# Second layer's head: moments, cleared buffers and first weight loads made in the stage in front, lone rows taken second

## What is computed

```python
x = x + L1(_gn(x), weight_real, weight_imag)

def _gn(v, G=32, eps=1e-5):                 # v seen as (B, H, W, C): C is the last axis, 128 wide
    g = v.reshape(B_, H_, W_, G, C_ // G)   # 32 groups of 4 columns
    m = jnp.mean(g, axis=(1, 2, 4), keepdims=True)
    s = jnp.var(g, axis=(1, 2, 4), keepdims=True)
    return ((g - m) / jnp.sqrt(s + eps)).reshape(v.shape)

def L1(x, wr, wi):
    weight = complex(wr, wi)                # (32 in, 32 out, 128, 65)
    x_ft = symmetric_padding(rfftshift(rfft2(x)))
    out_ft = einsum('bixy,ioxy->boxy', x_ft, symmetric_padding(weight))
    return irfft2(irfftshift(out_ft))
```

## Time and profile before

| what | value |
|---|---|
| device time, median of 3 runs | 1035.99 us (1034.77 to 1037.75) |
| device time of the profiled execution | 1040.15 us |
| its span in the profile | 1038.4 us |
| PE, DVE, ACT, POOL busy | 793.5, 677.6, 405.6, 319.4 us |
| stage 7 | 564.6 to 664.0 us |
| stage 8, head | 664.0 to 681.5 us |
| stage 8, loop | 681.5 to 957.6 us |
| stage 8, tail | 957.6 to 1038.4 us |
| mean granted clock of PE | 0.912 |

### The profile page before, as it was taken

The page is one execution under the profiler, slowest core; times in us unless marked ns, Lnnn a source line. Parts: engine busy times, 40 slices in busy tenths (PEclk is TensorE's granted clock), DMA queues, the critical chain, the costliest instruction groups (busy, mean ns, idle before and its releaser), DMA issues. The chain is left out here.

```text
span 1038.4 us, 37308 instructions
## 1 busy us (share of the span) xinstructions
PE 793.5 (76%) x16319; PEld 588.8 (57%) x16319; DVE 677.6 (65%) x1446; ACT 405.6 (39%) x919; POOL 319.4 (31%) x201
## 2 busy tenths in 40 slices
PE   0399496989999837999914999468777777776897
PEld 0366242222222217888703999457777777776786
DVE  4898499788888793566658999745555555552122
ACT  0199352222222263556533566333333333331121
POOL 0022375789999701111100000322222232210000
PEclk9999697999999978999956999888989899898899
DMA  9566643665556230554131676589999999998677
GB/s 366 110 188 174 139 90 108 242 219 170 196 161 194 86 79 22 167 125 117 39 75 40 167 200 176 117 180 252 287 283 289 283 283 281 286 283 175 197 235 218
DMA packets 284674, 189.45 MB, mean 182 GB/s; under 512 B 29397, under 2 KB 275894, under 8 KB 283382
## 3 DMA queue, kind: packets, MB, share of 16 engines
q1 hardware_dynamic: 207411, 139.95, 50.0%
q10 hardware_dynamic: 75138, 44.14, 16.9%
q0 software_dynamic: 2048, 4.36, 2.0%
HBM read 154.50 MB, written 33.07 MB: 181 GB/s over the span
## 5 line engine op out<-in xcount | busy, mean ns | idle before, releaser
L2101 PE MATMUL po<-pa,room 128*32 128x16 f32 x8320 | 146.6, 219 | 69.3 <-DMA room<-_L_conv_weight_imag_dram 44.7
L2101 PEld LDWEIGHTS po<-pa,room 128*32 128x32 f32 x8320 | 144.3, 162 | 76.9 <-issue 65.5
L1051 POOL TENSOR_TENSOR q<-lead 128x1536 f32<-128x1536 f32 (+1 forms) x49 | 163.5, 3364 | 19.7 <-PE acc L1088 17.0
L1134 DVE TENSOR_TENSOR q<-pw,lead 128x1536 f32<-128x1536 f32 (+1 forms) x84 | 139.0, 1703 | 15.8 <-PE acc L1088 13.9
L2054 POOL COPY cols<-y 128x512 f32<-128x512 f32 x32 | 36.8, 1149 | 326.3 <-PE px L2088 184.8
L1088 PE MATMUL acc<-q,pt 128*32 128x384 f32 (+1 forms) x1080 | 102.9, 493 | 12.2 <-DVE q L1134 12.2
L2242 DVE TENSOR_TENSOR osl<-po,neg 128x128 f32<-128x128 f32 x64 | 18.4, 288 | 132.9 <-ACT neg L2175 132.9
L2175 ACT ACTIVATE neg<-po 128x272 f32<-128x272 f32 x32 | 12.7, 398 | 180.5 <-issue 167.2
L2088 PE MATMUL px<-wbat,cols 128*32 128x130 f32 x2176 | 75.9, 291 | 3.7 <-DVE wbat L2213 3.0
L1088 PEld LDWEIGHTS acc<-q,pt 128*32 128x32 f32 x1080 | 27.9, 110 | 84.3 <-issue 54.8
L1446 PE MATMUL pz<-eh,ts 128*33 128x128 f32 x1024 | 66.3, 285 | 6.1 <-DMA ph<-const_ph_dram 3.8
(11 more groups left out here) (353 smaller groups left out, 1547.5 us busy)
## 6 DMA issues: line engine op xcount, KB each, us to landing
room<-_L_conv_weight_real_dram ACTq DMA_DIRECT2D x32, 520.0 KB, 8.6
room<-_L_conv_weight_imag_dram ACTq DMA_DIRECT2D x32, 520.0 KB, 11.3
room<-_L_conv_weight_real_dram SPq DMA_DIRECT2D x32, 520.0 KB, 6.4
room<-_L_conv_weight_imag_dram SPq DMA_DIRECT2D x32, 520.0 KB, 9.8
lead<-xns SPq DMA_DIRECT2D x64, 192.0 KB, 3.0
lead<-wv SPq DMA_DIRECT2D x16, 576.0 KB, 5.8
yall<-in_x_dram SPq DMA_DIRECT2D x4, 2048.0 KB, 14.6
xd<-in_x_dram SPq DMA_DIRECT2D x16, 512.0 KB, 4.1
```

Of the source, the lines that this page charges most:

```text
L1051: nc.gpsimd.tensor_tensor(q2[:, t % 2, :, :, 0:m], bc(weights(blk, n), 2, NB), spectra(blk), ALU.mult).then_inc(s_qp, 1)
L1134: V.tensor_tensor(q1[:, t % 2, :, :, 0:m], bc(pw[t % 4][:, 0:3 * m].rearrange("p (r m) -> p r m", r=3), 2, NB), spectra(blk), ALU.mult).th ...
L2101: e = nc.tensor.matmul(po[u][32 * g:32 * g + 32, 512 * q + 16 * m:512 * q + 16 * m + 16], wsl[u][:, :, q * KWF + KWF - 1 - kw], xsl[u][:, ...
```

## The change

Six edits, all in stages 7 and 8.

1. **Moments.** ACT's two sums of squares of a group now cover other elements: one the two columns 0 and 64 (16 elements a lane), one the rest (1008 elements a lane, scaled by the root of 2). Their accumulators then need only be added. At the end of stage 7 DVE makes both moments with two reductions; the ten steps of stage 8 are gone, and the factor 1/32 is in the constant `gmean`.
2. **Cleared buffers.** POOL clears `xsl` in stage 7, after the last `s_q7`.
3. **Matrices.** SP loads `gmean` and `wide` at the start of stage 7, ahead of that stage's own loads.
4. **First loads.** SP issues three of the eight first weight loads in stage 7, after the last read of `tt`; the other five follow at the start of stage 8, three on SP and two on ACT.
5. **First columns.** ACT instead of POOL copies the columns of the first chunk, one half on each side of its square root, and then issues its two loads; POOL copies those of the second chunk after `s_b0`.
6. **Order.** The chunk with the lone rows is taken second instead of last (`TURN8`).

```diff
+TURN8 = (0, NCHK - 1) + tuple(range(1, NCHK - 1))
...
-    c["gmean"] = (n[:, None] // 4 == n[None, :] // 4) / 4.0
+    c["gmean"] = (n[:, None] // 4 == n[None, :] // 4) / (4.0 * NT)
...
+        def load_weights(eng, p, c_, parts=(0, 1)):
+            u, k = c_ % 2, TURN8[c_]
+            if p == 1:
+                row0, step = HH // 2 - SL * (k + 1), 1
+            elif k < NCHK - 1:
+                row0, step = HH // 2 + 1 + SL * k, 1
+            else:
+                row0, step = HH // 2, HH // 2 - 1
...
             def _(sp):
+                for t, n in ((gmean, "gmean"), (wide, "wide")):
+                    sp.dma_start(t[:, :], c[n]).then_inc(s_ld, 16)
                 each_batch(body)
+                sp.wait_ge(s_ts, NGRP)
+                load_weights(sp, 0, 0)
+                load_weights(sp, 1, 0, (0,))
+
+            @block.gpsimd
+            def _(pool):
+                pool.wait_ge(s_q7, NGRP)
+                for v in range(2):
+                    nc.gpsimd.memset(xsl[v], 0.0).then_inc(s_zero, 1)
...
-                    act.activation(sq7[:, 0], y1[:, bass.ds(g * GI, GI), 0:64], ACT.Square, accum_out=en8[:, 0, bass.ds(g, 1)])
-                    act.activation(sq7[:, 1, :, 0:63], y1[:, bass.ds(g * GI, GI), 66:129], ACT.Square, accum_out=en8[:, 1, bass.ds(g, 1)]).then_inc(s_sq7, 1)
+                    act.activation(sq7[:, :, 126:128], y1[:, bass.ds(g * GI, GI), 0:65:64], ACT.Square, accum_out=en8[:, g, 0:1])
+                    act.activation(sq7[:, :, 0:126].rearrange("w i (s k) -> w i s k", s=2), y1p[:, g * GI:g * GI + GI, :, 1:64], ACT.Square, scale=ROOT2,
+                                   accum_out=en8[:, g, 1:2]).then_inc(s_sq7, 1)
...
+                dve.wait_ge(s_e1, NGRP)
+                V.reduce_sum(mo[:, 0, :], y1[:, :, 0].rearrange("w (b i) -> w b i", b=NB), axis=AX.X)
+                dve.wait_ge(s_sq7, NGRP)
+                V.reduce_sum(mo[:, 1, :], en8[:, :, :].rearrange("w (b q) s -> w b (q s)", b=NB), axis=AX.X).then_inc(s_mo8, 1)
...
             def _(sp):
-                for t, n in ((gmean, "gmean"), (wide, "wide")):
-                    sp.dma_start(t[:, :], c[n]).then_inc(s_ld, 16)
...
-                for c_ in range(NCHK):
+                load_weights(sp, 1, 0, (1,))
+                load_weights(sp, 0, 1)
+                for c_ in range(2, NCHK):
                     wait(sp, s_ms, c_ - 1)
                     load_weights(sp, 0, c_)
...
             def _(pool):
+                for c_ in range(1, NCHK + 2):
                     wait(pool, s_sp, c_ - 1)
                     if c_ < NCHK:
-                        near = y1v[:, SL * c_ + 1:SL * c_ + 3]
-                        if c_ == NCHK - 1:
+                        if c_ == 1:
                             pool.wait_ge(s_b0, 1)
...
             def _(act):
-                load_weights(act, 1, 0)
+                near, far = columns(0)
+                act.activation(cols[:, 0, 0:2], far, ACT.Copy)
+                root.serve(act, nc.scalar, gs[:, 2, :])
+                act.activation(cols[:, 0, 2:4], near, ACT.Copy).then_inc(s_col0, 1)
                 load_weights(act, 1, 1)
-                root.serve(act, nc.scalar, gs[:, 2, :])
                 act.wait_ge(s_zero, 2)
...
             def _(dve):
-                ch.link(V.reduce_sum(mo[:, 0, :], y1[:, :, 0].rearrange("w (b i) -> w b i", b=NB), axis=AX.X))
-
-                ch.link(V.tensor_tensor(sq[:, :, :], y1[:, :, 0:65:64], y1[:, :, 0:65:64], ALU.mult))
-                ch.link(V.reduce_sum(en2[:, :, :], sq[:, :, :].rearrange("w (b i) k -> w b k i", b=NB), axis=AX.X))
...
-                V.tensor_scalar(mo[:, :, :], mo[:, :, :], 1.0 / NT, None, ALU.mult).then_inc(s_mo8, 1)
...
-                    last = c_ == NCHK - 1
+                    last = TURN8[c_] == NCHK - 1
```

More of the change, by code:

```diff
@@ L1976, in build, with columns @@
             block = p8.enter_context(nc.Block())
+            y1v = y1[:, :, :].rearrange("w i (s k) -> w k s i", s=2)
+            def columns(c_):
+                k = TURN8[c_]
+                near = y1v[:, SL * k + 1:SL * k + 3]
+                return near, near if k < NCHK - 1 else y1v[:, 0:64:63]
             xob = xo.rearrange("(b o) h w -> h b o w", b=NB)
             yb = yall[:, :, :].rearrange("h (b o) w -> h b o w", b=NB)
[L1980 to L1996, removed]
             @block.sync
             def _(sp):
-                for t, n in ((gmean, "gmean"), (wide, "wide")):
-                    sp.dma_start(t[:, :], c[n]).then_inc(s_ld, 16)
                 def store_pairs(c_):
-                    u = c_ % 2
+                    u, k = c_ % 2, TURN8[c_]
                     sp.wait_ge(s_oc, c_ + 3)
@@ L2043, in _ @@
             def _(pool):
-                y1v = y1[:, :, :].rearrange("w i (s k) -> w k s i", s=2)
-                def columns(c_):
-                    u = c_ % 2
+                for c_ in range(1, NCHK + 2):
                     wait(pool, s_sp, c_ - 1)
                     if c_ < NCHK:
-                        near = y1v[:, SL * c_ + 1:SL * c_ + 3]
-                        if c_ == NCHK - 1:
+                        if c_ == 1:
                             pool.wait_ge(s_b0, 1)
-                        nc.gpsimd.tensor_copy(cols[:, u, 0:2], near if c_ < NCHK - 1 else y1v[:, 0:64:63])
-                        nc.gpsimd.tensor_copy(cols[:, u, 2:4], near).then_inc(s_col, 1)
-                    else:
-                        nc.gpsimd.memset(cols[:, u, 0, 0, 0:1], 0.0).then_inc(s_col, 1)
-                columns(0)
-                columns(1)
-                for v in range(2):
-                    pool.wait_ge(s_col, 2)
-                    wait(pool, s_zero, v)
-                    nc.gpsimd.memset(xsl[v], 0.0).then_inc(s_zero, 1)
-                pool.wait_ge(s_zero, 2)
-                for c_ in range(NCHK):
-                    columns(c_ + 2)
+                        near, far = columns(c_)
+                        nc.gpsimd.tensor_copy(cols[:, c_ % 2, 0:2], far)
+                        nc.gpsimd.tensor_copy(cols[:, c_ % 2, 2:4], near).then_inc(s_col, 1)
+                    else:
+                        nc.gpsimd.memset(cols[:, c_ % 2, 0, 0, 0:1], 0.0).then_inc(s_col, 1)
             @block.tensor
@@ L2074, in _, with spectrum @@
                 pe.wait_ge(s_wb, 1)
-                def spectrum(c_, u):
-                    pe.wait_ge(s_col, c_ + 1)
+                def spectrum(c_, u, first=False):
+                    if first:
+                        pe.wait_ge(s_col0, 1)
+                    else:
+                        pe.wait_ge(s_col, c_)
                     for q in range(SL):
@@ L2103, in mix @@
                     e.then_inc(s_ms, 1)
-                spectrum(0, 0)
+                spectrum(0, 0, True)
                 spectrum(1, 1)
```

53 lines of the change are left out of this document (27 added, 26 removed).

## The result

The changed kernel takes 1031.12 us against 1039.45 us of the kernel before (medians of 10 runs each, taken in turn on the same chip; 1025.9 to 1034.5 and 1034.8 to 1041.5). The ratio is 0.992 with a 95% interval of 0.9901 to 0.9939: 8.3 us less, between 6.3 and 10.3. A second session gave 0.9941 (0.9919 to 0.9963), 6.1 us less. Forecast were 9.2 us less. The 1035.99 of the first three runs was low for the kernel before, so the forecast time, 1026.8, lies 4.3 under the measured one although the difference of the first session fits.

The account below looks back on a forecast made before the run. The prediction took a chain of waits as the bound: the loop's DMA time is fixed, its start hangs on PE's first mix. 7.0 us at the head plus 2.2 at the end, 9.2, takes 1035.99 to 1026.8; range 1022.2 to 1032.2.

Parts of the forecast that it names:

- Stage 7's end: End of stage 7: new squares +0.05 us and DVE's sum +0.21, so stage 8 starts 0.26 later.
- the row of the scaling: Profile row of DVE's scaling held up by POOL's memset; applied to stage 7's last add, it means 1.8 us later.
- The three early loads: Weight loads moved into stage 7's idle DMA stretch: 5.3 us at 295 GB/s, worth nothing themselves but cover for the rest.
- The head: Start of stage 8 up to mix(0): 6.56 us from the group sum plus 0.45 from silent POOL, 7.0 earlier.
- The rival in which the clock stays up: Head of stage 8: PE's clock does not fall, mix(0) comes 1.8 us earlier, total 1025.0; chance 0.07.
- the wait for `s_b0`: POOL's new wait before copying chunk 1's columns: ready about 670.3, 0.9 us before spectrum(1) can start, so no delay.
- The first pass of the loop: From mix(0) on: everything that follows comes earlier by as much as mix(0) does, 7.0 us.
- an "issue" hole over 2 us in mix(0): Listed sign that the forecast is wrong: PE standing still in mix(0) over 2 us for reasons the profile calls issue.
- PE stalls longer in the first pass: Rival: code-fetch holes around mix(0) grow by 2.6 and 1.8 us, gain only 4.8, total 1031.2; chance 0.13.
- The loop's end: Last weight wait before mix(31): shorter by 1.5 to 4 us with the lone rows second, taken as 2.2.
- The shortening below an ordinary wait: Loop's end: last loads have the DMA engines to themselves, so the wait may come at most 2.2 us below ordinary.
- The change of pace: Rival: loop steps slow from 8.45 us, at 8.77 no gain is left, priced at 1045.2 total; chance 0.08.

Follow-up runs that it names:

- e8: Kernel before with only the moments changed and the two small matrices loaded in stage 7; ratio to the kernel before 0.9973.
- e1: Changed kernel with the order undone, so the chunk with the lone rows is last again; ratio to the kernel before 0.9957.
- e7: Changed kernel with the weight loads of chunks 1 and 2 cut to a thin strip, leaving DMA nearly idle; one run, read-back at 287.70 us.
- the repeat: Changed kernel measured again unaltered, in a second session; ratio to the kernel before 0.9941, read-back at 294.20 us.
- e2: Changed kernel with the moments undone (old squares, ten DVE steps in stage 8), POOL still silent there; ratio to the kernel before 0.9927.
- e5: Changed kernel with only POOL's two memsets put back at the start of stage 8; ratio to the kernel before 0.9933.
- e4: Changed kernel with six of the eight first weight loads in stage 7 instead of three; ratio to the kernel before 0.9944.
- e9: e8 with one line moved: ACT answers the root before its two loads of chunk 1; ratio to the kernel before 0.9958.
- e6: Changed kernel with five of the eight first weight loads in stage 7 instead of three; ratio to the kernel before 0.9932.
- e3: Changed kernel with the three early loads put back into stage 8, all on SP's queue; ratio to the kernel before 1.0047.

## Why the prediction was right, and where it was not

**Stage 7's end: right in sum.** Forecast was +0.26 for the start of stage 8, with the group sum at once behind it. The stage started 0.07 later and the group sum 0.2 after that, so that it gained 6.57 where 6.56 was forecast: two misses of 0.2 that cancel. The memsets cost DVE's add nothing, as forecast for its operand in PSUM; by the row of the scaling it would have been 1.8. This agrees with the Trainium skill, "SBUF — State Buffer", section "Who interferes with whom", by which such a DVE instruction does not collide with a GpSimd instruction that only writes SBUF. ACT's copies of the columns took 1.16 each, not 0.60; the forecast took the time of a read of adjacent values. They stayed covered. The three early loads took about 10 us (645.7 to 656) where 5.3 was forecast, since one queue alone reached about 180 GB/s and not 295; the idle stretch was long enough for that too.

**The head: right in size, with two terms that were luckier than argued.** 7.22 against 7.0 at the start of mix(0); the 0.2 is the group sum at the higher clock, which the forecast did not have. The rival in which the clock stays up did not come. But the forecast said nothing of ACT's queue, which e8 shows to be the first thing that a quick head runs into; the change takes it out by its edit 5, which I had costed at nothing. And it had costed the wait for `s_b0` by what it delays (right, it delays nothing) and not by what it keeps away from DVE (1.1, e1).

**The first pass of the loop: the step that failed.** The sum took the 7.0 at mix(0)'s start over to its end. It is 4.64 there and 5.0 behind mix(1), and the forecast's own sign of being wrong, an "issue" hole over 2 us in mix(0), came with 3.10. The rival "PE stalls longer in the first pass" had the mechanism at twice the size (4.4 more; measured 1.06 and 3.10 instead of 1.87, 2.3 more), with a chance of 0.13. That was too low: rows of before showed a short hole with idle and a long one with busy DMA engines, and the forecast itself kept them busy to 676 or later, over the middle of mix(0). The forecast did not have the second part of the loss, the lower clock behind the longer stall. The page of the Trainium skill that has code streaming ahead of use and mostly hidden ("Runtime: NRT & Kernel Launch", section "Instruction fetch mechanics") is not borne out in this first pass: even with idle DMA engines PE stands still four times for 0.9 to 1.7 us (e7).

**The loop's end: right side, too small.** 2.2 forecast, 2.8 by all kernels together and 3.6 in the pair compared; the difference of the two waits (1.8) is what the last wait gave (1.7). The shortening below an ordinary wait, which the forecast allowed for by the bytes, did not come in that wait (11.2, an ordinary one); the other 1.0 lies one step earlier and was not forecast.

**The loop itself: right.** From mix(1)'s end on, the gain is kept. The change of pace did not come: from the loads of chunk 3 to those of chunk 30 a step takes 8.41 before and 8.40 after.

**The sum.** 7.0 + 2.2 = 9.2 was forecast; 5.0 + 3.6 = 8.6 is what the profile shows up to the read-back, 8.1 in the repeat, and 8.3 and 6.1 the time of whole runs. So the sum is near because one term was 2 us too large and the other 0.6 too small (1.4 in the pair compared): that is luck. One slip stands in the chances: of the 0.08 for another pace half was put past the point of no gain, but 0.06 was then counted as slower. Left open: whether the tail is 1 us longer with the lone rows second. It takes 76.9 to 82.4 us there (80.2 on the mean of eight) and 78.3 to 79.7 (79.0 on the mean of four) in the others.

## What to carry to other kernels

When a chain of small steps on the way to a DMA-bound loop is cut short, ask what the next engine in line will be doing at the new time: here ACT was issuing loads into a full queue, PE then waited for the loads, and then, by the reading above, for its own code, and each had been hidden by the slow chain. The moments were worth 1.9 on the kernel before (e8) and 2.3 or less on the changed one (e2), the clears 0.5 or less (e5); the whole head brought 5. The early loads were not measured by themselves. And a wait of one engine can be worth its while for what it keeps that engine from doing beside another.

## What the runs showed of the hardware

- Each of PE's stalls in the first pass that was looked at ends 2.2 to 2.9 us after one packet of 0.02 MB on an instruction queue is moved (before, after, e2, e4, e9); with idle DMA engines it is 2.2 to 2.4 (e7). With idle DMA engines such a stall is 0.9 to 1.7 us in this loop's first pass (e7); with weights in flight up to 4.7 (e2).
- Behind a stall of 3.10 us PE's granted clock was 0.57 (after); behind one of 1.87 it stayed at 1.00 (before).
- A DVE step of 0.16 us on few values, with two operands in SBUF or as a scaling, waits for the end of a POOL copy (up to 1.05 us, e1 and e8); beside a memset the scaling waits (0.67, e5) and the step with two SBUF operands doesn't (0.16, e5). For two SBUF inputs the Trainium skill says the same in "SBUF — State Buffer", section "Who interferes with whom": they collide with a GpSimd instruction that reads SBUF, not with one that only writes it. Of the 3.8 us of waits in the moments before, 1.4 are of this kind and 2.4 are scalings.
- An issue of a 520 KB load takes 0.56 to 0.69 us as the first in its queue, 1.3 to 5.5 as the third in a row and 2.7 to 5.5 behind that (before, e4, e6, e8; 10.2 for one with runs of 260 bytes, e3). What stands behind it in that engine's list waits as long: SP's end of stage 7 in e4, ACT's root in e8.
- Runs of 260 bytes beside runs of 520: the last load took 12.9 instead of 11.2 us.
